# One clamp moved from VectorE to GpSimd in a 32-expert stage, and one wait made narrower

## The reference, cut to what matters

```python
def _swiglu(h):
    glu = jnp.minimum(h[..., ::2], LIMIT)            # LIMIT = 7.0
    lin = jnp.clip(h[..., 1::2], -LIMIT, LIMIT)
    return glu * jax.nn.sigmoid(ALPHA * glu) * (lin + 1.0)   # ALPHA = 1.702
h1 = jnp.einsum('th,efh->tef', tf, w1) + b1          # E = 32, H = F = 128
h = _swiglu(h1)
hw = h * combine[:, :, None]
out = jnp.einsum('tef,ehf->th', hw, w2) + combine @ b2
```

## Time and profile before

| | |
|---|---|
| runs | 6248.97 us median of 3 (6245.62 to 6252.19) |
| profiled execution, its own time | 6221.95 us |
| its span | 6220.1 us, 182529 instructions |
| busy share of the span | PE 84%, PEld 61%, DVE 57%, ACT 37%, POOL 40% |
| mean granted clock | 0.927 of full speed |
| the stage of 32 experts | 918 to 1750 us of the span |

### The profile page before, as it was taken

The page is one execution under the profiler, slowest core; times in us unless marked ns, Lnnn a source line. Parts: engine busy times, 40 slices in busy tenths (PEclk is TensorE's granted clock), DMA queues, the critical chain, the costliest instruction groups (busy, mean ns, idle before and its releaser), DMA issues. The chain is left out here.

```text
span 6220.1 us, 182529 instructions
## 1 busy us (share of the span) xinstructions
PE 5232.3 (84%) x72132; PEld 3776.6 (61%) x72132; DVE 3558.8 (57%) x9531; ACT 2288.6 (37%) x4072; POOL 2504.0 (40%) x2788
## 2 busy tenths in 40 slices
PE   4568868888848888898888888898679999787998
PEld 2334345555536777777777777777346666576776
DVE  4631268787865565555565565565545545685333
ACT  3532236666623333333333333333222333111333
POOL 1210014444436666666666666666300000573000
PEclk8789989999969999999999999999789999898999
DMA  0000010000000000000000000000010000000000
GB/s 19 2 20 0 2 42 1 0 0 0 0 7 11 11 11 12 12 13 12 11 12 11 11 12 11 11 12 11 7 42 0 0 0 0 4 1 28 0 0 13
DMA packets 29562, 58.05 MB, mean 9 GB/s; under 512 B 7312, under 2 KB 14240, under 8 KB 28704
## 3 DMA queue, kind: packets, MB, share of 16 engines
q1 hardware_dynamic: 28960, 48.86, 2.6%
HBM read 46.75 MB, written 2.10 MB: 8 GB/s over the span
## 5 line engine op out<-in xcount | busy, mean ns | idle before, releaser
L617 PEld LDWEIGHTS psum<-m_wd,m_h 128*128 128x128 f32 x6144 | 805.6, 192 | 485.4 <-issue 484.3
L617 PE MATMUL psum<-m_wd,m_h 128*128 128x128 f32 x6144 | 819.6, 277 | 95.3 <-remote 69.6
L2183 POOL TENSOR_TENSOR e_kd<-e_kd,e_tail 128x512 f32<-128x512 f32 x325 | 368.7, 1135 | 567.7 <-PE psum L2290 554.2
L607 PE MATMUL psum<-xT,m_wa 128*128 (+1 forms) x1032 | 544.3, 610 | 8.4 <-remote 8.4
L607 PE MATMUL psum<-xT,m_wb 128*128 (+1 forms) x1032 | 532.8, 598 | 0.0
L784 DVE SCALAR_TENSOR_TENSOR m_acc<-psum,m_combine,m_acc 128x128 f32<-128x128 f32 x1440 | 403.3, 342 | 224.0 <-PE psum L617 211.0
L544 POOL TENSOR_TENSOR m_h<-m_td,m_tb 128x512 f32<-128x512 f32 x258 | 328.6, 1274 | 468.6 <-DVE m_tb L812 468.6
L2320 PE MATMUL psum<-e_T,e_N 64*64 64x32 f32 x10400 | 407.1, 232 | 67.7 <-remote 66.3
L2320 PEld LDWEIGHTS psum<-e_T,e_N 64*64 64x64 f32 x10400 | 370.6, 148 | 113.2 <-issue 110.0
L2290 PE MATMUL psum<-e_kd,e_k 64*64 64x64 f32 x10400 | 420.1, 237 | 0.3
L143 POOL TENSOR_SCALAR m_post_rstd<-m_post_mv 128x4 f32<-128x4 f32 x27 | 6.2, 228 | 990.7 <-DVE m_post_mv L133 990.7
(11 more groups left out here) (434 smaller groups left out, 11884.4 us busy)
## 6 DMA issues: line engine op xcount, KB each, us to landing
e_w<-in_e_w SPq DMA_DIRECT2D x66, 321.0 KB, 2.9
m_wa<-in_m_wa SPq DMA_DIRECT2D x12, 512.0 KB, 7.5
m_wd<-in_m_wd SPq DMA_DIRECT2D x12, 512.0 KB, 8.7
m_wb<-in_m_wb SPq DMA_DIRECT2D x8, 512.0 KB, 8.8
f_h<-in_f_h SPq DMA_DIRECT2D x2, 1024.0 KB
out<-x SPq DMA_DIRECT2D x1, 2048.0 KB, 8.7
f_w<-in_f_w SPq DMA_DIRECT2D x3, 256.0 KB
g_w<-in_g_w SPq DMA_DIRECT2D x3, 256.0 KB
```

The lines of the kernel that those rows point to most:

```text
L607: pe.matmul(c.ps[i][:], w[q][:, j, :], xb, start=True, stop=True).then_inc(a_ready[i], 1)
L617: r = pe.matmul(c.ps[4 + e % 2][:, t * P:(t + 1) * P], h[:, u % DEPTH, t * P:(t + 1) * P], wd[u // UQ][:, u % UQ, :], start=(m == 0 and t ...
L2183: return g.tensor_tensor(both_odd(dst[:], m), both_odd(src[:], m), gate.unsqueeze(1).broadcast_to((P, 2, nb, m)), ALU.mult)
```

## The change

The in-place clamp of `tb` leaves VectorE's `front` and becomes a GpSimd instruction in front of the product, with a link between the two. Its wait is a new semaphore, `tb_ready`, which ScalarE's `tb` instruction raises. `t_ready`, which VectorE waits for, is now raised by the sigmoid, one ScalarE instruction earlier. `td_ready` is raised by the product `td` itself.

```diff
@@ hidden(u), on GpSimd
                 j = u % DEPTH
+                g.wait_ge(tb_ready[j], 1)
+                g.sem_clear(tb_ready[j])
+                ch.link(g.tensor_scalar(tb[:, j, :], tb[:, j, :], 8.0, 6.0, ALU.subtract, ALU.min))
                 g.wait_ge(td_ready[j], 1)
                 g.sem_clear(td_ready[j])
                 g.tensor_tensor(h[:, j, :], td[:, j, :], tb[:, j, :], ALU.mult).then_inc(h_ready[j], 1)
@@ front(u), on ScalarE
-                a.activation(tc[:, j, :], ta[:, j, :], ACT.Sigmoid, scale=-1.702, bias=c1[:])
+                a.activation(tc[:, j, :], ta[:, j, :], ACT.Sigmoid, scale=-1.702,
+                             bias=c1[:]).then_inc(t_ready[j], 1)
                 a.wait_ge(a_ready[2 * k + 1], 1)
                 a.sem_clear(a_ready[2 * k + 1])
                 a.activation(tb[:, j, :], c.ps[2 * k + 1][:], ACT.Relu, bias=bb[:, u:u + 1],
-                             scale=-1.0).then_inc(t_ready[j], 1)
+                             scale=-1.0).then_inc(tb_ready[j], 1)
@@ front(u), on VectorE
-                    v.scalar_tensor_tensor(td[:, j, :], ta[:, j, :], 7.0, tc[:, j, :], ALU.subtract, ALU.mult)
-                    v.tensor_scalar(tb[:, j, :], tb[:, j, :], 8.0, 6.0, ALU.subtract, ALU.min).then_inc(td_ready[j], 1)
+                    v.scalar_tensor_tensor(td[:, j, :], ta[:, j, :], 7.0, tc[:, j, :], ALU.subtract,
+                                           ALU.mult).then_inc(td_ready[j], 1)
```

More of the change, by code:

```diff
@@ L517, in stage_moe @@
     td_ready = [s(f"td{i}_ready") for i in range(DEPTH)]
+    tb_ready = [s(f"tb{i}_ready") for i in range(DEPTH)]
     y_ready = [s(f"y{i}_ready") for i in range(2)]
```

## The result

The changed kernel takes 6356.02 us (median of 4, 6348.44 to 6361.01), the kernel before beside it 6247.3 us. The ratio is 1.0179, 95% interval 1.0162 to 1.0196: 109 us slower. Forecast was 6250 us, with a range up to 6295 us.

A forecast was written before the change was run, and what follows sets the result against it. It took PE as near its end (busy 91.2 of 104 us), VectorE close behind. Per batch 1.2 + 1.1 us gained and 2.4 paid made 0.8 us slower in eight: 6222.8 profiled, plus 27.0, rounded to 6250 us; range 6215 to 6295.

The forecast's parts named there:

- The price of GpSimd's clamp: GpSimd's 128x512 clamp in the 32-expert loop: taken as 0.66 us, between a copy's 0.61 and a two-input product's 1.27.
- The formula for a dear clamp: Per unit: 0.55 us of VectorE's product, clamp, 0.08 link, 1.27 GpSimd product; times 32, plus rstd pairs and extras.
- The first rival: GpSimd's clamp is dearer than a copy: 0.94 us gives 6276 us, the product's 1.27 gives 6361; chance 0.36.
- The turns: VectorE's L811 and GpSimd's clamp and product exclude each other at SBUF: 2.56 us per unit, just below PE's 2.61.
- Gains and turns cancel: Per batch of the 32-expert loop, gains at PE's stalls are offset by blocked VectorE work: 0.1 us slower.
- the blocked pieces: VectorE instructions at `AT_ADD`, `AT_LN2`, `AT_LN3` held up by GpSimd: 1.2, 0.2 and 1.0 us per batch.
- 2.3 gained, 2.4 paid: Per batch: 1.2 us at the loop head and 1.1 at the router gained; 2.4 paid at three blocked places.
- The slack of a collect: Time VectorE's collect has before PE's `down` needs its bank: 1.16 us in the even part, growing by 0.9 to 2.1.
- Over 0.8, the first rival: Sign in the profile after: GpSimd's 128x512 tensor_scalar at 0.66 us; over 0.8 would mean the clamp is dearer than a copy.
- L811 0.8 to 1.1 us: Sign: VectorE's product, 0.69 us before, grows to 0.8 to 1.1 us in the mean, where GpSimd is in its turn.
- L155 above 0.588: Sign: VectorE's instruction at L155 takes longer than its 0.588 us in this loop.
- 2.8 or more: Sign: PE's step in the even part stays 2.61 us; 2.8 or more means the turn has become the bound.

The follow-up runs named there:

- run with two subtractions: Changed kernel with a two-input subtraction of a constant tile in place of GpSimd's clamp, minimum and true constant left out: 6296.69 us in one run.
- narrow wait: Against the kernel before: VectorE's product waits for the sigmoid alone; the clamp stays on VectorE with its own wait for `tb`: 6219.3 us, ratio 0.9952.
- cut pieces: Product waiting for the sigmoid alone, clamp on VectorE, VectorE's four largest extra pieces cut in two, second half one unit later: 6207.42 us; measured again, 6199.24 us.
- odd units: Product waiting for the sigmoid alone, clamp on GpSimd for the 16 odd units, on VectorE for the even ones: 6257.92 us, ratio 1.0020 to the kernel before.

## Why the prediction was wrong, step by step

- **The price of GpSimd's clamp is the step that failed.** With it failed the statement that GpSimd needs 2.0 us per unit, under PE's 2.61. The prediction took 0.66 us "because the clamp reads one tensor like the copy", and as its upper bound the two-input product's 1.27. It measured 1.92 undisturbed and 2.00 in the mean, outside both ends. The bound was no bound: it supposed that the number of inputs sets GpSimd's time, while the first operation put 0.88 us on top of the copy's 0.61 and the second another 0.43. The 228 against 185 ns at four columns was carried over as a fixed 0.04 us; at 512 columns the difference was thirty times that. With the length measured, GpSimd needs 1.92 + 0.18 + 1.27 + 0.08 = 3.45 us per unit (the link is 0.18 us, not 0.08), and it is the bound.
- **The formula for a dear clamp was wrong as well.** It puts VectorE's product, the clamp and GpSimd's product end to end. With 1.92 us in it the turn is 3.82 us and a batch 32 x 3.82 + 3.9 + 5.7 + 3.2 + 3 = 138.0 us, which is 6527 us. GpSimd alone, 32 x (2.00 + 1.29 + 0.26) = 113.6 us plus three rstd pairs, 4, gives 117.6 of the measured 118.6. The first rival, with a chance of 0.36, was right that the clamp is dearer. It priced the product's 1.27 us at 6361 us by adding turns; the time came out as 6356 us, but for another reason: no turn of VectorE's product lies in the 3.45 us step. The agreement is chance.
- **The turns are real, their size was wrong for the clamp.** The Trainium skill ("SBUF — State Buffer", Who interferes with whom) has the two instructions exclude each other for the whole instruction. The run with two subtractions agrees: VectorE's product ends 0.55 us after GpSimd's, and the turn is 3.12 us against 3.17 reckoned. GpSimd's two-operation clamp does not: in the section below VectorE is let in after 0.60 us of its 1.92. In the changed kernel GpSimd's instructions are longer than undisturbed by (2.00 - 1.92) + (1.29 - 1.27) = 0.10 us per unit, so an estimate of what the turns cost is 3.2 us per batch, 26 in eight; GpSimd's own time is the rest.
- **Gains and turns cancel: only in part.** With a copy of 0.61 us in the clamp's place the prediction's sum can be tried. It said 103.5 us per batch and 6250; 101.7 and 6213.64 were measured, just below the range that the prediction gave (from 6215). GpSimd's extra instruction and the relief of VectorE did cancel (101.7 against 101.5). The narrow wait is worth 2.1 us per batch by itself (103.6 to 101.5), and the prediction let it be eaten by the blocked pieces: 2.3 gained, 2.4 paid, where 1.9 was left over. Whether the gain was taken too small or the payment too large, no run separates.
- **The slack of a collect.** No run measures the 1.16 us, nor the 0.6 us more from the earlier product. That the cut pieces shorten the batch by 1.2 us fits stalls that come when a piece is longer than the slack. It is less than the 2 to 4 us expected, so part of the stalls hangs on something else, perhaps the sum of VectorE's work or the loop head; this was not tried.
- **Signs given in advance.** "Over 0.8, the first rival" was the right sign. "L811 0.8 to 1.1 us" was not: 0.765. "L155 above 0.588" was not either: 0.410, which fits a long clamp that leaves the path free for most of its time. "2.8 or more" for PE's step came, with 3.45 us, but it was to mean that the turn had become the bound, and the bound was GpSimd's own time.

## What to carry to other kernels

An engine with half its time idle is no free place until the operation's own length there is measured: here 0.42 us on VectorE became 1.92 us on GpSimd, and 32 of them filled the idle engine and made it the bound. Bound an unseen instruction by the operations it does per element as well as by its inputs, and work out the queue of the engine that receives it: clamp + product + gaps against the step of the bound engine would have said at once from which price on it loses (2.61 - 1.27 - 0.26 = 1.08 us, an estimate from below, since GpSimd may fall behind a little and catch up: 1.30 us in the mean on half the columns cost 0.5 us per batch against the narrow wait alone, 1.61 with one operation cost 8). An instruction moved into the chain to the bound engine can also make its data late while the receiving engine has room, as the odd units show. Split a change into its parts: a wait on less than everything was worth 0.5% here, and was hidden under a move that cost 1.8% by itself.

## What the runs showed of the hardware

GpSimd's one-input tensor_scalar on 128x512 float32 takes 1.92 us with subtract and min, 1.49 with subtract alone, against 0.61 for a copy and 1.27 for a two-input product. The Trainium skill ("GPSIMD Engine Reference", Engine selection) calls one-input work roughly line rate. The copy's 0.84 ns per column may pass for that, the clamp's 3.3 ns do not, and here the measurement decides.

The long clamp does not hold the path to SBUF for its whole length. Timeline of the changed kernel:

```profile
1167.36 1.93 POOL L545 TENSOR_SCALAR m_tb<-m_tb 128x512 f32<-128x512 f32 x1
...
1167.68 0.84 DVE L816 SCALAR_TENSOR_TENSOR m_td<-m_ta,m_tc 128x512 f32<-128x512 f32 x1 [0.26 <-remote]
```

L816, with both inputs in SBUF, starts 0.32 us into the clamp, takes 0.84 us instead of 0.69, and ends 0.77 us before the clamp does. Taking off the 0.55 us that its data need, it was let in 1.92 - 0.77 - 0.55 = 0.60 us after the clamp's start, which is the length of a plain copy. GpSimd's product, in the run with two subtractions, let it in only at its end. Two more traces show what the 0.60 us hangs on, first with one operation, then with two on 256 columns:

```profile
1108.51 1.49 POOL L545 TENSOR_SCALAR m_tb<-m_tb 128x512 f32<-128x512 f32 x1
1108.74 0.92 DVE L816 SCALAR_TENSOR_TENSOR m_td<-m_ta,m_tc 128x512 f32<-128x512 f32 x1 [0.26 <-remote]
```

```profile
1397.71 1.07 POOL L545 TENSOR_SCALAR m_tb<-m_tb 128x256 f32<-128x256 f32 x1
1397.74 0.91 DVE L816 SCALAR_TENSOR_TENSOR m_td<-m_ta,m_tc 128x512 f32<-128x512 f32 x1 [0.26 <-ACT m_tc L714]
```

In the first, VectorE's product ends 1.15 us after the clamp's start, as in the changed kernel (1.16), although the clamp is 0.43 us shorter: let in after 0.60 us. In the second it ends 0.94 us after it: let in after 0.39 us, and a copy of 256 columns would take 0.40 by the slope of the earlier trace rows. So the time for which the path is held goes with the columns and not with the operations. That GpSimd has read its input by then and works on fits this, but it is an inference; no run shows the reads themselves.
